# Thirty units projected beside the determinants and fetched on the even steps of the mixing stage

## The reference, cut to what matters

```python
value = silu(conv(x W_in))                         # (B, T, 256)
bc = einsum('bti,oi->bto', value, W_bc)            # (B, T, 32 heads, 4, 32)
bc = bc / (norm(bc, axis=-1) + EPS)                # Bz, Bx, Cz, Cx
S = 1 / (1 + dt*k + dt*dt*A)
z = S*(z - dt*A*s + dt*(Bz*u));  s = s + dt*z + dt*(Bx*u)      # step over T
y = Cz.z + Cx.s
```

## Time and profile before

| what | us |
|---|---|
| three runs, median | 1347.55 (1346.82 to 1349.2) |
| the profiled execution, its own time | 1347.47 |
| its span, first to last instruction | 1345.7 |
| front(), to the last copy of `ent` | 0 to 210 |
| mix() | 211 to about 652 |
| the MLPs and attention | about 652 to 1346 |

### The profile page before, as it was taken

The page is one execution under the profiler, slowest core; times in us unless marked ns, Lnnn a source line. Parts: engine busy times, 40 slices in busy tenths (PEclk is TensorE's granted clock), DMA queues, the critical chain, the costliest instruction groups (busy, mean ns, idle before and its releaser), DMA issues. The chain is left out here.

```text
span 1345.7 us, 22918 instructions
## 1 busy us (share of the span) xinstructions
PE 1274.0 (95%) x7806; PEld 706.0 (52%) x7806; DVE 908.2 (67%) x1771; ACT 635.2 (47%) x1536; POOL 590.2 (44%) x939
## 2 busy tenths in 40 slices
PE   7999668999999999998799998999999999999999
PEld 4443224566566566655445445555555556544545
DVE  6999997888988998989301205888787787630100
ACT  3266214555565565565322314666565666532221
POOL 2633314878878878888300001444344354500000
PEclk7999899999999999999899999999999999999999
DMA  2368896555555555557200002000000000000000
GB/s 82 156 258 334 312 398 235 194 181 184 195 183 184 185 185 192 185 185 234 67 0 0 0 0 89 1 2 1 1 1 1 1 1 1 1 1 0 16 0 16
DMA packets 67746, 143.50 MB, mean 107 GB/s; under 512 B 6833, under 2 KB 22833, under 8 KB 64817
## 3 DMA queue, kind: packets, MB, share of 16 engines
q1 hardware_dynamic: 63024, 129.47, 27.3%
q10 hardware_dynamic: 4608, 12.58, 2.4%
HBM read 94.58 MB, written 47.45 MB: 106 GB/s over the span
## 5 line engine op out<-in xcount | busy, mean ns | idle before, releaser
L1806 POOL TENSOR_SCALAR pr<-pr,rs,sg 128x512 f32<-128x512 f32 (+3 forms) x256 | 152.7, 612 | 204.8 <-DVE rs L1711 185.9
L648 PE MATMUL banks<-w_bc,valueT 128*128 128x512 f32 x448 | 210.7, 594 | 2.1 <-DVE pp L986 2.1
L986 DVE TENSOR_TENSOR pp<-banks,rec 128x1024 f32<-128x1024 f32 x128 | 156.1, 1220 | 6.0 <-POOL bp L1082 0.3
L1612 ACT ACTIVATE pr<-banks,nm 128x512 f32<-128x512 f32 (+3 forms) x256 | 132.8, 524 | 20.5 <-DVE nm L1705 17.7
L1705 DVE TENSOR_REDUCE nm<-banks 128x2 f32<-128x1024 f32 (+3 forms) x128 | 105.5, 824 | 4.4
L648 PEld LDWEIGHTS banks<-w_bc,valueT 128*128 128x128 f32 x448 | 76.7, 190 | 59.7 <-issue 55.5
L1600 ACT COPY prT<-banks 128x512 f32<-128x512 f32 (+3 forms) x128 | 54.3, 424 | 112.5 <-PE banks L1481 112.2
L1067 POOL TENSOR_SCALAR_AFFINE_SELECT bp<-bp 128x1024 f32<-128x1024 f32 x64 | 73.6, 1150 | 75.8 <-ACT bp L880 75.3
L1321 DVE TENSOR_TENSOR x<-x,banks 128x256 f32<-128x256 f32 x16 | 6.7, 421 | 148.3 <-PE banks L1232 148.3
L873 ACT COPY qk<-banks 128x512 f32<-128x512 f32 x128 | 75.0, 586 | 64.0 <-PE banks L773 64.0
L1481 PE MATMUL banks<-ident,pr 128*128 128x128 f32 x640 | 96.9, 281 | 2.1 <-POOL pr L1806 0.7
(11 more groups left out here) (240 smaller groups left out, 2420.5 us busy)
## 6 DMA issues: line engine op xcount, KB each, us to landing
rec<-psi SPq DMA_DIRECT2D x126, 512.0 KB, 4.5
psi<-X SPq DMA_DIRECT2D x15, 2048.0 KB, 7.2
det<-w_bc ACTq DMA_DIRECT2D x16, 512.0 KB, 5.0
dd<-det SPq DMA_DIRECT2D x64, 128.0 KB, 4.7
bcs<-xp ACTq DMA_DIRECT2D x16, 256.0 KB, 6.4
w_bc<-in_w_bc SPq DMA_DIRECT2D x4, 1024.0 KB, 11.1
back<-bcs SPq DMA_DIRECT2D x16, 256.0 KB, 5.0
w_bc<-in_f_h SPq DMA_DIRECT2D x4, 1024.0 KB, 7.8
```

Source lines behind the costliest of these rows:

```text
L648: mm = pe.matmul(bank, m["valueT"][:, c, t * P:(t + 1) * P], w, start=(c == 0), stop=(c == 1))
L986: dve.tensor_tensor(pp[:, q % 2].rearrange("p (a c) n -> p a c n", c=2), sc.unsqueeze(2).broadcast_to([P, 4, 2, HN]), rec[:, n % RL, q % 2 ...
L1612: act.activation(pr[:, n % RP, h, 0:w], S[n % 2][:, h, 0:w], ACT.Exp, bias=nm[:, n % 4, h:h + 1], accum_out=sm[:, m % 3, n % 2, h:h + 1]). ...
L1806: pool.tensor_scalar(row, row, rs[:, n // 2 % 2, n % 2, h:h + 1], sg[:, TPB * b + it, hd:hd + 1], ALU.mult, ALU.mult).then_inc(s["scaled"], 1)
```

## The change

Thirty units instead of 16 are projected in front(): units 8t+5 and 8t+1 for t = 1 to 15. The units 7, 15, ... 127 are projected in mix() again. In the order of making, `MADE`, the fifteen units 8t+5 come first and then the fifteen 8t+1. The first 16 are made inside the loop of the determinants, one behind each (PE `prepare`, ACT `keep`), in banks 6 and 7 instead of 2 and 3; the other 14 behind the loop. Two head groups need two weight tiles: `wp` and, borrowed, `sq`. The store buffers are four instead of two, in the memory of `ent`, so ACT waits for their stores ahead of the first copy of `ent`. The pieces of w_bc that share no memory with the determinants are loaded at blocks 8 and 9, the others at blocks 13 and 14; the wait for the stored determinants moves from block 10 to block 13. In mix() not a line changes: the units 8t+5 and 8t+1 are the second of their pairs and fall on p = 4t-2 and p = 4t-4, even steps.

```diff
-PREPARED = list(range(7, TILES * HG, HG))
-RPRE = 2
+MADE = [HG * t + 5 for t in range(1, TILES)] + [HG * t + 1 for t in range(1, TILES)]
+PREPARED = sorted(MADE)
+RPRE = 4
...
-        pre = after[:, 0:RPRE * 4 * HN].rearrange("p (r c) -> p r c", r=RPRE)
+        pre = m["ent"][:].rearrange("p t f c -> p (t f c)")[:, 0:RPRE * 4 * HN].rearrange("p (r c) -> p r c", r=RPRE)
...
-        BC_LOADS = (10, 12, 13, 14)
+        BC_LOADS = {8: (0, 1), 9: (1, 1), 13: (0, 0), 14: (1, 0)}
-        wp = sb("wp", P, 2, 4 * G4 * N)
+        wp = [sb("wp", P, 2, 4 * G4 * N), m["sq"]]
...
             for i in range(NBLK):
-                if i == 10:
-                    for r in range(2):
-                        sp.wait_ge(d_stored[r], 16 * TILES // 2)
+                if i == 8:
                     sp.wait_ge(s["conv"], 2 * B)
...
+                if i == 13:
+                    for r in range(2):
+                        sp.wait_ge(d_stored[r], 16 * TILES // 2)
                     last = scratch["det"][:, P - 1, :].rearrange("t (g f) -> g t f", g=HG)
...
+            def prepare(e):
+                t, f, j = split(MADE[e])
+                if e < 2:
+                    pe.wait_ge(s["wp_loaded"], 64)
+                    pe.wait_ge(s["u"], TILES // 2 - 1 + e)
+                else:
+                    pe.wait_ge(s["pre_taken"], e - 1)
+                for c in range(2):
+                    w = wp[1 - f][:, c].rearrange("p (i c n) -> p c i n", i=4, c=4)
+                    mm = pe.matmul(BGB[e % 2][:], m["valueT"][:, c, t * P:(t + 1) * P], w, start=(c == 0), stop=(c == 1))
+                mm.then_inc(s["pre_ready"], 1)
...
                         pe.matmul(LGB[q][:], ones_le[:], lng[:, (t - 1) % 2, q * 512:(q + 1) * 512]).then_inc(s["LG"], 1)
-            pe.wait_ge(s["wp_loaded"], 32)
-            for e, q in enumerate(PREPARED):
...
+                    prepare(t - 1)
+            for e in range(TILES, len(MADE)):
+                prepare(e)
             pe.wait_ge(bc_loaded[0], 32)
+            pe.wait_ge(s["lng"], 2 * TILES)
+            pe.wait_ge(s["pre_taken"], len(PREPARED))
...
+            def keep(e):
+                r = e % RPRE
+                act.wait_ge(s["pre_ready"], e + 1)
+                if e >= RPRE:
+                    act.wait_ge(pre_stored[r], 16 * (e // RPRE))
+                act.copy(pre[:, r], BGB[e % 2][:]).then_inc(s["pre_taken"], 1)
+                act.wait_ge(s["pre_taken"], e + 1)
+                act.dma_start(scratch["bcs"][PREPARED.index(MADE[e])], pre[:, r]).then_inc(pre_stored[r], 16)
...
                 det_exp(t)
-            for e in range(len(PREPARED)):
...
+                keep(t)
+            for e in range(TILES, len(MADE)):
+                keep(e)
...
+            for r in range(RPRE):
+                act.wait_ge(pre_stored[r], 16 * len(range(r, len(PREPARED), RPRE)))
```

More of the change, by code:

```diff
@@ L137, in front @@
         after = xp[:].rearrange("p b t -> p (b t)")
-        pre = after[:, 0:RPRE * 4 * HN].rearrange("p (r c) -> p r c", r=RPRE)
-        pick = after[:, RPRE * 4 * HN:RPRE * 4 * HN + 2 * TILES * 4 * DH].rearrange("p (f t e) -> p f t e", f=2, t=TILES)
+        pre = m["ent"][:].rearrange("p t f c -> p (t f c)")[:, 0:RPRE * 4 * HN].rearrange("p (r c) -> p r c", r=RPRE)
+        pick = after[:, 0:2 * TILES * 4 * DH].rearrange("p (f t e) -> p f t e", f=2, t=TILES)
         s = {n: sem("fr_" + n) for n in (
@@ L190, in _ @@
             sp.dma_start(scratch["psi"][:, 0, :], X[:, SLOTS - 1, :]).then_inc(s["id_stored"], 16)
-            _, pf_, pj_ = split(PREPARED[0])
             wide = ins["w_bc"].rearrange("(c p) (f i j a) -> p c f j i a", p=P, f=2, i=4, j=4)
-            for c in range(2):
-                sp.dma_start(wp[:, c].rearrange("p (i a) -> p i a", i=4), wide[:, c, pf_, pj_]).then_inc(s["wp_loaded"], 16)
+            for n in range(2):
+                f, j = split(MADE[-n])[1:]
+                for c in range(2):
+                    sp.dma_start(wp[n][:, c].rearrange("p (i a) -> p i a", i=4), wide[:, c, f, j]).then_inc(s["wp_loaded"], 16)
             for i in range(NBLK):
-                if i == 10:
-                    for r in range(2):
-                        sp.wait_ge(d_stored[r], 16 * TILES // 2)
+                if i == 8:
                     sp.wait_ge(s["conv"], 2 * B)
@@ L206, in _ @@
                 if i in BC_LOADS:
-                    f, c = divmod(BC_LOADS.index(i), 2)
+                    f, c = BC_LOADS[i]
                     o = slice(f * HG // 2 * 4 * HN, (f + 1) * HG // 2 * 4 * HN)
@@ L438, in _ @@
             pe.wait_ge(s["phi"], 4)
-            pe.wait_ge(s["pre_taken"], len(PREPARED))
+            pe.wait_ge(s["D"], 2 * TILES)
             for n in range(LINKS // 2):
```

## The result

The changed kernel takes 1415.78 us in the median of six runs (1410.57 to 1424.94), the kernel before 1347.97 beside it: a ratio of 1.0497, 95% interval 1.0456 to 1.0538. It is slower, as forecast (1376.4), but by 68 us where 29 were forecast, and outside the range (1333 to 1386). Lines behind the edit are shifted by 14: L648 is now L662, L963 L977, L986 L1000, L999 L1013, L1005 L1019, L1014 L1028, L1067 L1081, L1087 L1101, L784 L798, L815 L829. The run of the front alone, further down, had two slow executions in ten (2206 and 7155 us, the first of them the profiled one), which are left out of its ratio, and its trace isn't read.

A forecast was written before the change was run, and what follows sets the result against it. It took DVE's recurrence to bound front(), with PE arriving together, and PE to bound mix() almost everywhere. Terms +32, -4.6 and +1.5 gave +28.9 on 1347.5, so 1376.4 us; range 1333 to 1386.

The forecast's parts named there:

- Front: In front(), the 14 late units and their stores stay nearly covered by DVE's recurrence; +1.5 us.
- Its rival: In front(), the 14 late units wait for stores while mix() comes out even; +7 us, 1354.5 us, chance 0.07.
- The even and the odd step: In mix(), fetching shortens the even step by 1.76 us, so the odd one starts at X + 5.24, not X + 7.00.
- X: Start of scores in the even step of a pair of mix() steps; offsets in us count from it.
- POOL's gap: In mix(), 1.7 us between POOL's last combining and next mask, where DVE's state operations ran; said to vanish.
- The collision: In mix()'s odd step, DVE's state operations meet POOL's mask and combinings: +1.4 us a pair, +32 over 23 pairs.
- What follows the late projection: In mix(), PE's work from the odd step's late projection to the next step takes 3.5 us, giving 15.0 a pair.
- The term for the pairs without a state: In mix(), seven fetching pairs that update no state each save about 0.65 us; -4.6 in all.
- No collision: Rival: in mix() the state finds POOL free, pairs take 13.3 us, -7.6 in all; 1336.8 us, chance 0.17.
- PE as the bound everywhere: Rival: PE sets the pace throughout mix(), so its full saving of 35.5 us shows; 1312 us, chance 0.12.

The follow-up runs named there:

- The run of the front alone: Changed kernel's front() with 30 stored units, but mix() fetches only 16, on odd steps as the kernel before did; ratio 1.0013 to the kernel before.
- The run with a PSUM operand: Changed kernel with DVE's four state operations reading one operand from PSUM instead of SBUF (result no longer the state); 1347.47 us, ratio 0.9965 to the kernel before.
- the run with the state moved: Changed kernel with DVE's four state operations moved behind the products of unit 2p+7; 1354.49 us, ratio 1.0028 to the kernel before.
- The filler run: Changed kernel with two unread matmuls ahead of the second projection, only on odd steps whose pair updates a state; 1389.31 us, ratio 1.0317 to the kernel before.

## Why the prediction was right and wrong

*Front: right.* Forecast +1.5, measured +1.8, with the loop's end at 166 (169 forecast) and the last units waiting a little for stores. Its rival got 0.07; the run of the front alone excludes it as the rule, though the late stores of two executions of later runs, 8 to 10 us beyond this one, are what it described.

*The even and the odd step: right.* X + 5.24 forecast, X + 5.28 measured; POOL free at X + 7.64, measured 7.66; mask and state together there. POOL's gap vanished as read.

*The collision: right, in kind and size.* Products from X + 10.2 forecast, 10.40 measured; projection at X + 11.5, measured 11.66. One operation behind the mask and two behind combinings: 1.11, 0.69 and 0.81 measured. The run with a PSUM operand shows the cause, the run with the state moved shows the path by which it costs.

*What follows the late projection: wrong.* The step that failed is "From that project to the next step are 3.59 today, some tenths less where there is no project_out; I take 3.5: 15.0 a pair against 13.63". It took the duration of PE's work from rows at a clock of 1.00, for a place right behind a stall of 2.4 us. There the granted clock falls in 18 of the 23 pairs, and 3.59 became 5.38 in steps 8 and 9. The filler run, which has the collision but not the fall, gives 15.29 for the pair that was forecast at 15.0: +1.7 instead of +1.4, so 39 of the 67.6 us are the forecast's term of 32, a little short, and 28 are the clock. The rows to foresee it were at hand: the earlier trace rows show a mean clock of 0.88 in a stretch in which PE stood still again and again, and I read that row for its transfers alone. The first of those stalls is 2.67 us long, and the window behind it is at the lower level throughout; PE and windows of the trace before:

```profile
150.81 8.83 PE L432 MATMUL banks<-wp,valueT 128*128 128x512 f32 x16 [2.67 <-ACT xp L555]
```

```profile
151.00:153.00 2.00, 2.00 (x3) 0.97 (x4) 2.00 (x8) 0.59 (x1) 0.55 (x2) 0.50 0.53 192
```

*The term for the pairs without a state* was forecast at -4.6, as seven times 0.65, and measured at -4.1. That is luck: the six inside give 0.24 each, -1.4 together, and pair 0/1 gives 2.7 by itself. *The start of mix()* had no term and costs 2.9 us; no run takes it apart.

*The rivals.* "No collision" is what the PSUM run measures: 13.3 a pair forecast, 13.54 measured. Part of that is a slip in the sum, since 6.5 + 3.34 + 0.05 is 9.89 and not 9.8; the run projects at X + 9.90, and the slip made -7.6 of what should be about -5.5. That run came out at 0.9965 of before, so even with most of the collision gone fetching on even steps would hardly have paid; its price of 1336.8 was 11 us too low. PE as the bound everywhere was never near: even in the PSUM run PE still waits 0.66 for the products of DVE, and the pair stays at 13.5.

| term | forecast | measured |
|---|---|---|
| front | +1.5 | +1.8 |
| 23 pairs with a state, products late | +32 | +39 |
| the same pairs, clock behind the stall | none | +28 |
| pairs without a state | -4.6 | -4.1 |
| start of mix() | none | +2.9 |
| sum | +28.9 | +68 |

The range failed mainly for the same reason: its upper end took the collision near its worst, but no term for what a stall does to PE's own instructions. Not only for it: the filler run, without the clock's fall, is at 1389.31, still 3 us over the upper end, by the two small terms that were short or missing (+39 for +32, and the start).

## What to carry to other kernels

Taking work off the bounding engine moves every other engine's work in time. Ask of each short instruction which gap it lives in and whether the gap survives; two engines can collide over an operand, with no wait between them in the code. Price a stall of PE that is new not only by its length but also by PE's work behind it at the lower clock, from a stretch of the same trace where PE stands still, and give the case that the clock holds a chance: it held in 5 of 23 pairs here. And where a removed piece should be taken from is as important as how much: here the same thirty units gave -9 us on odd steps and +68 on even ones.

## What the runs showed of the hardware

- An operation of 128x128 float32 on DVE with both operands in SBUF took 1.11 us in the middle of POOL's mask, and 0.29 us with one operand in PSUM at the same moment. Against a chain of POOL operations of 0.73 to 0.77 each it took 0.69 to 0.81. A copy of 128x64 from SBUF took 1.14 us beside the mask and 0.18 away from POOL's work.
- A stall of 2.41 us of PE in an otherwise full stage was followed by a granted clock of 0.74 and 0.72 over some 6 us. Of 23 such stalls, of 1.98 to 2.99 us, 18 were followed by a fall and five by none, one of these 2.98 us long. With stalls of 0.66 to 1.60 us (the PSUM run) it stayed at 1.00. Two unread matmuls of 128x512 in the stall kept it at 1.00 and made the kernel 26 us faster.
- Fourteen more stores of 256 KB beside a running recurrence raised the queues' mean from 361 to 384 GB/s and delayed the end by 1.8 us in this execution, by 8 to 10 more in two of nine.
